# Four chained layers on one core: a second DMA queue, group norm 0 image by image, four attend banks, and setup work placed beside the convolution

## The chip, the core and the metric

One core of one Trainium2 chip runs the whole program. TensorE (PE) multiplies, VectorE (DVE) and ScalarE (ACT) work on rows of 128 partitions, GpSimd (POOL) does the roots and some elementwise work, SyncE (SP) starts transfers. The metric is the device time of one execution in microseconds; lower is better.

## The reference

The input x has 4 images of 128 channels and 16 by 16 pixels. Four layers are added to it one after another, each fed with a group norm of the running sum (32 groups of 4 channels, per image):

```
x = x + attention(gn(x))        # L0: q, k, v, softmax over 256 x 256 scores, output weights
x = x + binary_conv(gn(x))      # L1: batch norm, sign, grouped 3x3 conv with sign weights, batch norm, residual, prelu
x = x + depthwise_block(gn(x))  # L2: 3x3 depthwise conv, bn, relu, prune, 1x1 conv, bn, relu, prune
x = x + linear_attention(gn(x)) # L3: softmax(k) over pixels, context per head, output weights
```

The batch norms of L1 take mean and variance over all four images, so that each of them is a point where all images meet.

## The kernel before, in words

Everything is float32 except the operands of the binary convolution and of the filler matmuls. Channels lie on the partitions, an image is 256 columns. Each engine has one list of instructions written out by hand, and works through it in order; semaphores tie the lists together. So a wait at the head of an engine's list holds all that is behind it.

The start. SP issues four transfers on one queue: image 0, images 1 to 3 together, the early parameters (attention weights), the late parameters. DVE takes the statistics of image 0 (L722, L726, L730), PE averages them over the groups with a small matmul (L1198, `group_means`), DVE reads the result (L737, `group_out`) and forms the variance (L744), POOL takes the root (L321), DVE normalises (L750). Images 1 to 3 go through the same steps as one batch (L770 to L786, `other_group_means`, `other_roots`). On DVE the statistics of image 1 stand ahead of `group_out` of image 0.

Layer 0. For each image PE projects q, k and v (L1230, L1237, L1247), makes the scores (L1259), transposes the exponentials (L1270) and multiplies them with v (`attend`, L1283); ACT copies and exponentiates, DVE takes row maxima (L838) and adds the result to x (`x1_out`, L853). Attends 0, 1 and 2 write the same PSUM bank, so attends 1 and 2 wait until the image ahead was read by DVE.

Filler. `keep_warm(n)` is n bf16 matmuls of 256 columns whose result nobody reads (L1180).

Constants. ACT makes nine diagonal matrices of depthwise weights (`dw_diagonal`, L487) among the first steps. PE multiplies each with a mask of ones inside the image (`valid_taps`, L1310), which gives, for each pixel, the sum of the depthwise weights that fall inside; ACT copies that to `valid_sum` (`valid_taps_out`, L492). The mean of the group norm, times `valid_sum`, is taken off the depthwise result later (`mean_taps_out`, L565). `valid_taps` and images 0 and 2 of the depthwise convolution share bank 3, and `depthwise(0)` on PE begins with

```
                pe.wait_ge(x2_ready, b + 1)
                if b == 0:
                    pe.wait_ge(valid_ready, 1)
```

Layer 1. `norm1`, the first batch norm (L869 to L913), the signs (ACT, L524), four convolutions of nine taps (PE, L1296), their statistics (DVE, L919), the second batch norm, `bn2_apply` (ACT, L531), then DVE `h1_out` (L934), ACT `negative_part` (L537), DVE `x2_out` (L943).

Layer 2. PE does five taps of the depthwise convolution (L1324), ACT two (`act_tap`, L554), DVE two (L961); `group_means(2, b)` stands behind `depthwise(b)` on PE, and `group_out(2, 0)` ahead of DVE's taps and of `x2_out(3)`. Layers 2 and 3 behind that are not touched by the change.

Of the kernel before, what the change touches and what calls it, by code (L numbers as in the profile page):

```python
# [20 lines left out]
N = H * W  # L21
# [29 lines left out]
def build(nc, x, early, late, out):  # L51
# [10 lines left out]
    with ctx:  # L62
# [121 lines left out]
        o_ps = [banks[i][:, 0:N] for i in (6, 6, 6, 1)]  # L184
        setup_ps = banks[6]
# [14 lines left out]
        x_in = [sem("x_in0"), sem("x_in1")]  # L200
# [32 lines left out]
        exp_ready = sem("exp_ready")  # L233
# [52 lines left out]
        def _(pool):  # L286
# [37 lines left out]
            pool.wait_ge(var_ready[0], 1)  # L324
            root(rstd[:, 0, 0:1], ve[:, 0, 0:1]).then_inc(rstd_ready[0], 1)
            pool.wait_ge(early_in, 16)
            for i, name in enumerate(("bv", "bo")):
                ins = nc.gpsimd.tensor_scalar(bias_rows[:, i, :], ones[:, :], ep[:, EC[name]], 0.0,
                                              ALU.mult, ALU.add)
            ins.then_inc(pool_consts, 1)  # L330

            def other_roots():
                pool.wait_ge(var_ready[0], 2)
                root(rstd[:, 0, 1:B], ve[:, 0, 1:B]).then_inc(rstd_ready[0], 1)

            def x_bias(b):

                pool.wait_ge(setup_done, 2)
                pool.wait_ge(x_in[min(b, 1)], 16)
# [101 lines left out]
            x1_res_out(3)  # L441
            bn_root(1)
# [25 lines left out]
        def _(act):  # L468
            act.wait_ge(early_in, 16)
            nc.scalar.activation(bq_s[:, :], ep[:, EC["bq"]], ACT.Copy, scale=SCALE).then_inc(setup_done, 1)  # L470
            act.wait_ge(late_in, 16)
            nc.scalar.activation(conv_sign[:, :, :],
                                 lp[:, LC["conv_in"]].rearrange("p (t o) -> p t o", t=TAPS),
                                 ACT.Sign).then_inc(conv_sign_ready, 1)

            def setup_out():

                act.wait_ge(setup_mm, 1)
                nc.scalar.activation(setup[:, :, :].rearrange("p a c -> p (a c)"), setup_ps[:, 0:2 * C],
                                     ACT.Copy).then_inc(setup_done, 1)  # L480

            def dw_diagonal(tap):

                if tap == 0:
                    act.wait_ge(pool_consts, 1)
                at = LC["dw"].start + tap
# [13 lines left out]
            def softmax(b):  # L500
                act.wait_ge(nmax_ready, b + 1)
                for par in range(2):
                    nc.scalar.activation(prob[:, b, par, :], s_ps[b % 2][:, par * N:(par + 1) * N],  # L503
                                         ACT.Exp, bias=nmax[:, b, par:par + 1],
                                         accum_out=psum_rows[:, b, par:par + 1]).then_inc(exp_ready, 1)
# [101 lines left out]

            act.wait_ge(setup_done, 1)
            dw_diagonal(0)
# [3 lines left out]
            q_out(0)  # L613
# [3 lines left out]
            setup_out()  # L617
            dw_diagonal(7)
            dw_diagonal(8)
            v_out(0)  # L620
            q_out(1)
            softmax(0)
            q_out(2)
            v_out(1)
            q_out(3)
            softmax(1)
            prob_out(0)
            softmax(2)
            prob_out(1)
            softmax(3)  # L630
            prob_out(2)
            v_out(2)
            v_out(3)
            prob_out(3)
            sign_out(0)
            valid_taps_out()
            sign_out(1)
            sign_out(2)
            sign_out(3)
# [12 lines left out]
            negative_part(3)  # L652
            square_sum(2, 1)
# [43 lines left out]
        def _(dve):  # L697
# [57 lines left out]
            dve.wait_ge(x_in[0], 16)  # L755
            gn_stats(0, 0)
            gn_aggr(0, 0)
            gn_mean_sq(0, 0)
            dve.wait_ge(x_in[1], 16)
            gn_stats(0, 1)  # L760
            dve.wait_ge(pool_consts, 1)
            group_out(0, 0)
            gn_stats(0, 2)
            group_var(0, 0)
            gn_stats(0, 3)
            for b in range(1, B):
                gn_aggr(0, b)
            normalise(0, 0, t0[:, 0, :], 1)
            settle("aggr", 0, B - 1)
            step(nc.vector.tensor_tensor(msq0[:, 1:B], mv[:, 0, 1:B, 0], mv[:, 0, 1:B, 0], ALU.mult),  # L770
                 "msq0")
            settle("msq0")
            nc.vector.tensor_tensor(mv[:, 0, 1:B, 2], mv[:, 0, 1:B, 1], msq0[:, 1:B],
# [766 lines left out]
```

## Time and profile before

| | us |
|---|---|
| median of 3 runs | 76.61 |
| the 3 runs | 76.24, 78.25, 76.61 |
| span of the profiled execution, first to last instruction | 75.0 |
| PE busy, share of the span | 61.9 (83%) |
| DVE busy | 51.8 (69%) |
| ACT busy | 39.5 (53%) |
| POOL busy | 37.7 (50%) |

The page gives the profiled execution's own time as its span alone; the three runs carry no profile. The median is 1.6 us above the span. A row of the timeline gives the start, the duration, the engine, the line, the operation with its output and inputs, how many were merged, and in brackets how long the engine had been idle and what ended it.

### The profile page before, as it was taken

The numbers are of one execution on the slowest core, as the hardware profiler recorded it, in microseconds if no ns is written. First come the engines' busy times: TensorE is split into PE (matmuls) and PEld (weight loads), VectorE is DVE, ScalarE is ACT, GpSimd is POOL, SyncE is SP. The second block draws the span as 40 slices with busy tenths as digits, with TensorE's granted clock in tenths as the row PEclk, the third lists the DMA queues.
The fourth block names the chain that finished last, engine by engine and source line by source line (L and its number), as shares of the span: only waits on it lengthen the run. The fifth ranks groups of instructions, "written<-read, shape, count | busy, mean of one in ns | idle before, by whom it ended". The sixth has DMA issues, their size and how long they took to land.

```text
span 75.0 us, 1268 instructions
## 1 busy us (share of the span) xinstructions
PE 61.9 (83%) x371; PEld 50.9 (68%) x371; DVE 51.8 (69%) x179; ACT 39.5 (53%) x114; POOL 37.7 (50%) x81
## 2 busy tenths in 40 slices
PE   3993889799999999069999439949998999999930
PEld 2762778498999776046788238838775879899810
DVE  3919859674689979802262994999999998743530
ACT  5103884758945000092003889976548597977410
POOL 6605999889604547900003975999991334200000
PEclk9999999999999999975799999999999999999997
DMA  0692000000000000000000000000000000002222
GB/s 4 162 395 81 0 0 0 0 0 4 0 0 9 4 0 0 0 4 0 0 9 0 0 0 0 0 0 0 0 0 0 0 0 0 4 9 70 70 70 70
DMA packets 1415, 1.81 MB, mean 24 GB/s; under 512 B 128, under 2 KB 1152, under 8 KB 1408
## 3 DMA queue, kind: packets, MB, share of 16 engines
q1 hardware_dynamic: 1408, 1.73, 7.0%
q8 instruction: 3, 0.05, 0.2%
q14 instruction: 4, 0.03, 0.2%
HBM read 1.20 MB, written 0.52 MB: 23 GB/s over the span
## 4 chain that ended last, share of the span: by engine, by line
PE 33%; DVE 23%; issue 18%; POOL 13%; DMA 6%; ACT 3%; SPq 1%; POOLq 0%; ACTq 0%
DMA x<-in_x 6%; PE bank L1259 4%; DVE t L750 3%; PE bank L1324 3%; POOL gn_rstd L321 3%; PE bank L1347 3%; PE bank L1405 3%; POOL dw_rest L398 3%; PE bank L1385 3%; PE bank L1283 3%; DVE x L853 2%; DVE dw_acc L961 2%; POOL x_res L414 2%; PE bank L1270 2%; PE bank L1365 2%
## 5 line engine op out<-in xcount | busy, mean ns | idle before, releaser
L321 POOL TENSOR_TENSOR gn_rstd<-gn_var_eps,minus_half 128x1 f32<-128x1 f32 (+1 forms) x14 | 9.1, 651 | 13.5 <-DVE gn_var_eps L744 13.4
L1324 PE MATMUL bank<-x,dw_diag 128*128 128x256 f32 x40 | 9.5, 385 | 2.2 <-DVE x L943 2.2
L1180 PE MATMUL bank<-warm 128*128 128x256 bf16 x67 | 10.3, 314 | 1.2 <-POOL warm L306 1.2
L1324 PEld LDWEIGHTS bank<-x,dw_diag 128*128 128x128 f32 x40 | 7.3, 189 | 3.4 <-DVE x L943 2.5
L1180 PEld LDWEIGHTS bank<-warm 128*128 128x128 bf16 x67 | 7.4, 113 | 2.9 <-POOL warm L306 1.2
L1296 PE MATMUL bank<-signs,conv_blocks 128*128 128x256 bf16 x36 | 5.9, 338 | 2.6 <-ACT signs L524 2.6
L1296 PEld LDWEIGHTS bank<-signs,conv_blocks 128*128 128x128 bf16 x36 | 4.2, 118 | 4.4 <-issue 3.0
L524 ACT ACTIVATE signs<-res,bn_shift,bn_scale 128x256 bf16<-128x256 f32 x4 | 2.2, 598 | 8.2 <-DVE bn_shift L913 8.2
L919 DVE BATCH_NORM_STATS2 bn_stats<-bank 128x6 f32<-128x256 f32 x4 | 1.7, 432 | 5.4 <-PE bank L1296 5.4
L321 POOL TENSOR_TENSOR bn_rstd<-bn_var_eps,minus_half 128x1 f32<-128x1 f32 x2 | 1.2, 602 | 8.4 <-DVE bn_var_eps L929 7.8
L531 ACT ACTIVATE bn_out<-bank,bn_shift,bn_scale 128x256 f32<-128x256 f32 x4 | 2.0, 558 | 6.4 <-DVE bn_shift L913 6.4
L750 DVE TENSOR_SCALAR t<-x,gn_group,gn_rstd 128x256 f32<-128x256 f32 x8 | 4.4, 567 | 0.9 <-POOL gn_rstd L321 0.8
L1310 PE MATMUL bank<-valid,dw_diag 128*128 128x256 f32 x18 | 4.5, 388 | 0.0
L722 DVE BATCH_NORM_STATS2 gn_stats<-x 128x6 f32<-128x256 f32 x8 | 3.3, 416 | 1.7 <-DMA x<-in_x 1.7
L1259 PE MATMUL bank<-k,q 128*128 128x256 f32 x16 | 4.3, 389 | 0.2 <-DVE k L833 0.2
L1283 PE MATMUL bank<-vt,probT 128*128 128x128 f32 x32 | 4.4, 280 | 0.0
L420 POOL TENSOR_TENSOR x_h<-bn_out,x_res 128x256 f32<-128x256 f32 x4 | 3.6, 917 | 1.5 <-ACT bn_out L531 1.5
L503 ACT ACTIVATE prob<-bank,nmax 128x256 f32<-128x256 f32 x8 | 3.7, 476 | 0.8 <-DVE nmax L838 0.8
L1283 PEld LDWEIGHTS bank<-vt,probT 128*128 128x128 f32 x32 | 3.9, 192 | 0.0
L1198 PEld LDWEIGHTS bank<-gn_mean_sq,group_sum 128*128 128x128 f32 x16 | 2.6, 188 | 1.8 <-ACT squares L546 1.5
L744 DVE SCALAR_TENSOR_TENSOR gn_var_eps<-gn_group 128x1 f32<-128x1 f32 x13 | 3.6, 278 | 0.1
L838 DVE TENSOR_REDUCE nmax<-bank 128x2 f32<-128x512 f32 x4 | 2.8, 688 | 1.4 <-PE bank L1259 1.4
(151 smaller groups left out, 169.3 us busy)
## 6 DMA issues: line engine op xcount, KB each, us to landing
out<-x SPq DMA_DIRECT2D x4, 128.0 KB, 1.7
late_params<-in_late SPq DMA_DIRECT2D x1, 404.5 KB, 4.8
x<-in_x SPq DMA_DIRECT2D x1, 384.0 KB, 4.1
early_params<-in_early SPq DMA_DIRECT2D x1, 258.0 KB, 4.3
x<-in_x SPq DMA_DIRECT2D x1, 128.0 KB, 2.0
```

Of the source, the lines that this page charges most:

```text
L321: return nc.gpsimd.tensor_tensor(out_ap, in_ap, minus_half[:, 0:n], ALU.pow)
L420: nc.gpsimd.tensor_tensor(x1_h1[:, b, :], bn2_out[:, b, :], x1_res[:, b, :], ALU.add).then_inc(x1_h1_ready, 1)
L503: nc.scalar.activation(prob[:, b, par, :], s_ps[b % 2][:, par * N:(par + 1) * N], ACT.Exp, bias=nmax[:, b, par:par + 1], accum_out=psum_ro ...
L722: step(nc.vector.bn_stats(st[:, layer, b, :], xs[layer][:, b, :]), "stats", layer, b)
L744: nc.vector.scalar_tensor_tensor(out=ve[:, layer, b:b + 1], in0=g[:, 0:1], scalar=g[:, 0:1], in1=g[:, 1:2], op0=ALU.mult, op1=ALU.subtract ...
L750: nc.vector.tensor_scalar(dst, xs[layer][:, b, :], gs[:, layer, b, 0:1], rstd[:, layer, b:b + 1], ALU.subtract, ALU.mult).then_inc(t_ready ...
L1180: nc.tensor.matmul(bank[:, 0:N], warm[:, 0:C], warm[:, :], start=True, stop=True)
L1259: ins = nc.tensor.matmul(s_ps[b % 2][:, par * N:(par + 1) * N], q[:, b, par:N:2], k[:, b, :], start=True, stop=True)
L1283: ins = nc.tensor.matmul(o_ps[b][:, par * C:(par + 1) * C], probT[:, b, j, par, :], vt[:, b, j, :], start=(j == 0), stop=(j == 1))
L1296: ins = nc.tensor.matmul(conv_ps[b], conv_w[:, tap, :], signs[:, b, dy:dy + H, dx:dx + W], start=(tap == 0), stop=(tap == TAPS - 1))
L1310: ins = nc.tensor.matmul(valid_ps, dw_diag[:, tap, :], valid[:, dy:dy + H, dx:dx + W], start=(tap == 0), stop=(tap == TAPS - 1))
L1324: ins = nc.tensor.matmul(dw_ps[b], dw_diag[:, tap, :], xs[2][:, b, dy:dy + H, dx:dx + W], start=(tap == 0), stop=(tap == PE_TAPS - 1))
```

## The change

Five edits, with no change in what is computed.

1. ACT issues the early parameters on its own queue as its first instruction; SP issues image 0, image 1, images 2 and 3, and the late parameters.
2. Group norm 0 runs image by image with the same helpers as the other layers. The batch of three is gone.
3. Attends 0 to 3 write banks 6, 0, 1 and 2, so none waits for DVE's read of the one ahead; they wait for the last q, k or v to leave the bank. The softmax steps and transposes are split by halves and reordered, and the lists of PE, ACT and DVE in layer 0 are written anew.
4. The weights' fold and the bias' fold are two PSUM banks and two ACT copies.
5. Setup moves: the nine diagonals on ACT and the scale of the binary weights on DVE go behind the signs, `valid_taps` on PE behind the four convolutions, `valid_taps_out` on ACT behind `negative_part(3)`; POOL's masks and layer-2 constants go behind `x1_res_out(3)`. Filler stands where the taps were: 8, 3 and 32 ahead of the convolution, 12 instead of 33 behind.

The core of the diff:

```diff
-        o_ps = [banks[i][:, 0:N] for i in (6, 6, 6, 1)]
-        setup_ps = banks[6]
+        o_ps = [banks[i][:, 0:N] for i in (6, 0, 1, 2)]
+        fold_ps = banks[6][:, 0:C]
+        bias_ps = banks[5][:, 0:C]
...
-            sp.dma_start(xs[0][:, 1:B, :], x_v[1:B].rearrange("b c n -> c b n")).then_inc(x_in[1], 16)
-            sp.dma_start(ep[:, :], early).then_inc(early_in, 16)
+            sp.dma_start(xs[0][:, 1, :], x_v[1]).then_inc(x_in[1], 16)
+            sp.dma_start(xs[0][:, 2:B, :], x_v[2:B].rearrange("b c n -> c b n")).then_inc(x_in[2], 16)
             sp.dma_start(lp[:, :], late).then_inc(late_in, 16)
...
-            valid_mask()
-            head_masks()
-            other_roots()
+            gn_root(0, 0)
+            bias_broadcast()
+            gn_root(0, 1)
+            gn_root(0, 2)
+            gn_root(0, 3)
             x_bias(0)
             x_bias(1)
+            conv_weights()
             x_bias(2)
             x_bias(3)
-            l2_constants()
-            conv_weights()
-            sw_root()
...
             x1_res_out(2)
             x1_res_out(3)
+            valid_mask()
+            sw_root()
+            l2_constants()
+            head_masks()
             bn_root(1)
...
         def _(act):
+            act.dma_start(ep[:, :], early).then_inc(early_in, 16)
             act.wait_ge(early_in, 16)
...
+            sign_out(0)
+            sign_out(1)
+            sign_out(2)
+            sign_out(3)
             dw_diagonal(0)
...
             negative_part(3)
+            valid_taps_out()
             square_sum(2, 1)
...
             bn_shift_out(0)
+            sw_stats()
+            sw_aggr()
+            sw_variance()
+            sw_abs_sum()
             bn2_stats(0)
+            sw_scale()
+            sw_products()
...
                 pe.wait_ge(v_ready, b + 1)
                 pe.wait_ge(pt_ready, b + 1)
-                if b == 3:
+                if b == 1:
+                    pe.wait_ge(q_ready, B)
+                elif b == 2:
                     pe.wait_ge(k_ready, B)
-                elif b >= 1:
-                    pe.wait_ge(x1_ready, 2 * b)
+                elif b == 3:
+                    pe.wait_ge(v_ready, B)
...
             attend(3)
+            pe.wait_ge(exp_ready[1], B)
+            keep_warm(8)
+            group_means(1, 2)
+            keep_warm(3)
+            group_means(1, 3)
+            keep_warm(32)
+            conv(0)
+            conv(1)
+            conv(2)
+            conv(3)
             valid_taps(0)
             valid_taps(1)
-            group_means(1, 2)
             valid_taps(2)
-            group_means(1, 3)
...
             valid_taps(8)
-            conv(0)
-            conv(1)
-            conv(2)
-            conv(3)
-            keep_warm(33)
+            keep_warm(12)
             depthwise(0)
```

How the instructions move, at three places.

PE around the convolution (`bank<-valid` are the `valid_taps`, `bank<-signs` the convolution, `bank<-warm` filler, `bank<-x,dw_diag` the depthwise taps). Before:

```order
L1198 MATMUL bank<-gn_mean_sq,group_avg 128x2 [waits group_read1,stats_ready1]
L1310 MATMUL bank<-valid,dw_diag 128x256 [waits dw_diag_ready] x6
L1296 MATMUL bank<-signs,conv_blocks 128x256 [waits sign_ready,conv_w_ready]
L1296 MATMUL bank<-signs,conv_blocks 128x256 x8
...
L1296 MATMUL bank<-signs,conv_blocks 128x256 [waits sign_ready]
L1296 MATMUL bank<-signs,conv_blocks 128x256 x8
L1180 MATMUL bank<-warm 128x256 x33
L1324 MATMUL bank<-x,dw_diag 128x256 [waits valid_ready,x2_ready]
```

And now:

```order
L1204 MATMUL bank<-gn_mean_sq,group_avg 128x2 [waits group_read1,stats_ready1]
L1186 MATMUL bank<-warm 128x256 x32
L1303 MATMUL bank<-signs,conv_blocks 128x256 [waits sign_ready,conv_w_ready]
L1303 MATMUL bank<-signs,conv_blocks 128x256 x8
...
L1303 MATMUL bank<-signs,conv_blocks 128x256 [waits sign_ready]
L1303 MATMUL bank<-signs,conv_blocks 128x256 x8
L1317 MATMUL bank<-valid,dw_diag 128x256 [waits dw_diag_ready,exp_ready_odd,sum_masks]
L1317 MATMUL bank<-valid,dw_diag 128x256 [waits dw_diag_ready] x8
L1186 MATMUL bank<-warm 128x256 x12
L1331 MATMUL bank<-x,dw_diag 128x256 [waits valid_ready,x2_ready]
```

The taps of the mask went from ahead of the convolution to behind it, filler took their place, and the depthwise convolution waits for `valid_ready` as it did.

ACT from the signs to layer 2 (`valid_sum` is the copy that gives `valid_ready`, `h_neg` the negative part). Before:

```order
L524 ACTIVATE signs<-res,bn_shift,bn_scale 128x16x16 [waits t_ready1,bn_shift_ready,borders]
L492 ACTIVATE valid_sum<-bank 128x256 [waits valid_mm]
L524 ACTIVATE signs<-res,bn_shift,bn_scale 128x16x16 [waits t_ready1] x3
L531 ACTIVATE bn_out<-bank,bn_shift,bn_scale 128x256 [waits bn_shift_ready]
L531 ACTIVATE bn_out<-bank,bn_shift,bn_scale 128x256 x2
L537 ACTIVATE h_neg<-h 128x256 [waits h1_ready] x3
L531 ACTIVATE bn_out<-bank,bn_shift,bn_scale 128x256
L546 ACTIVATE squares,gn_mean_sq<-x 128x256 [waits x2_ready]
L554 ACTIVATE act_taps<-x,late_params 128x256 [waits x2_ready] x4
L537 ACTIVATE h_neg<-h 128x256 [waits h1_ready]
```

And now:

```order
L531 ACTIVATE signs<-res,bn_shift,bn_scale 128x16x16 [waits t_ready1,bn_shift_ready,borders]
L531 ACTIVATE signs<-res,bn_shift,bn_scale 128x16x16 [waits t_ready1] x3
L495 ACTIVATE dw_diag<-ident,late_params 128x128 [waits late_in,pool_consts]
L495 ACTIVATE dw_diag<-ident,late_params 128x128 x8
L538 ACTIVATE bn_out<-bank,bn_shift,bn_scale 128x256 [waits bn_shift_ready]
L538 ACTIVATE bn_out<-bank,bn_shift,bn_scale 128x256 x2
L544 ACTIVATE h_neg<-h 128x256 [waits h1_ready] x3
L538 ACTIVATE bn_out<-bank,bn_shift,bn_scale 128x256
L553 ACTIVATE squares,gn_mean_sq<-x 128x256 [waits x2_ready]
L561 ACTIVATE act_taps<-x,late_params 128x256 [waits x2_ready] x4
L544 ACTIVATE h_neg<-h 128x256 [waits h1_ready]
L500 ACTIVATE valid_sum<-bank 128x256 [waits valid_mm]
```

The copy to `valid_sum` moved from behind the first sign to behind the fourth `h_neg`, past sixteen instructions.

DVE in group norm 0 (`gn_group` is the read of the group means, `t` the normalised image). Before:

```order
L722 BN_STATS gn_stats<-x 128x6 [waits x_in1]
L737 TENSOR_TENSOR gn_group<-bank,eps_row 128x2 [waits group_ready0,pool_consts]
L722 BN_STATS gn_stats<-x 128x6
L744 SCALAR_TENSOR_TENSOR gn_var_eps<-gn_group 128x1 [waits group_read0]
L722 BN_STATS gn_stats<-x 128x6
L726 BN_AGGR gn_mean_sq<-gn_stats 128x2 [waits dve_step] x3
L750 TENSOR_SCALAR t<-x,gn_group,gn_rstd 128x256 [waits rstd_ready0]
L770 TENSOR_TENSOR gn_mean_squared<-gn_mean_sq 128x3 [waits dve_step]
L773 TENSOR_TENSOR gn_mean_sq<-gn_mean_sq,gn_mean_squared 128x3 [waits dve_step]
...
L778 TENSOR_TENSOR gn_group<-bank,eps_row 128x6 [waits group_ready0]
L783 TENSOR_TENSOR gn_mean_squared<-gn_group 128x3 [waits group_read0]
L786 TENSOR_TENSOR gn_var_eps<-gn_group,gn_mean_squared 128x3 [waits dve_step]
```

And now:

```order
L750 TENSOR_TENSOR gn_group<-bank,eps_row 128x2 [waits group_ready0,pool_consts]
L757 SCALAR_TENSOR_TENSOR gn_var_eps<-gn_group 128x1 [waits group_read0]
L735 BN_STATS gn_stats<-x 128x6 [waits x_in1]
L739 BN_AGGR gn_mean_sq<-gn_stats 128x2 [waits dve_step]
L743 SCALAR_TENSOR_TENSOR gn_mean_sq<-gn_mean_sq 128x1 [waits dve_step]
L763 TENSOR_SCALAR t<-x,gn_group,gn_rstd 128x256 [waits rstd_ready0]
L735 BN_STATS gn_stats<-x 128x6 [waits x_in23]
L750 TENSOR_TENSOR gn_group<-bank,eps_row 128x2 [waits group_ready0]
L739 BN_AGGR gn_mean_sq<-gn_stats 128x2 [waits dve_step]
L757 SCALAR_TENSOR_TENSOR gn_var_eps<-gn_group 128x1 [waits group_read0]
L743 SCALAR_TENSOR_TENSOR gn_mean_sq<-gn_mean_sq 128x1 [waits dve_step]
L814 TENSOR_SCALAR k<-bank,early_params 128x256 [waits k_mm]
```

The read of image 0's group means no longer stands behind the statistics of image 1, and images 1 to 3 have their own chain each.

## Rows read from the trace of the kernel before

**Rows 1.** The page's granted clock in forty slices, and its chain that ended last.

```profile
PEclk9999999999999999975799999999999999999997
...
PE 33%; DVE 23%; issue 18%; POOL 13%; DMA 6%; ACT 3%; SPq 1%; POOLq 0%; ACTq 0%
```

**Rows 2.** Timeline of the start: start us, us, engine, line, operation.

```profile
0.80 0.38 SPq L276 DMA_DIRECT2D x<-in_x  x1
...
1.72 0.48 SPq L278 DMA_DIRECT2D early_params<-in_early  x1
...
3.50 0.22 DVE L730 SCALAR_TENSOR_TENSOR gn_mean_sq<-gn_mean_sq 128x1 f32<-128x1 f32 x1
...
5.41 0.43 DVE L722 BATCH_NORM_STATS2 gn_stats<-x 128x6 f32<-128x256 f32 x1 [1.69 <-DMA x<-in_x]
...
5.75 0.14 DVE L737 TENSOR_TENSOR gn_group<-bank,eps_row 128x2 f32<-128x2 f32 x1
...
6.10 0.30 PEld L1205 LDWEIGHTS bank<-early_params 128*128 128x128 f32 x2 [0.94 <-DMA early_params<-in_early]
...
8.07 0.68 PE L1230 MATMUL bank<-t,early_params 128*128 128x256 f32 x2
...
10.60 2.27 DVE L750 TENSOR_SCALAR t<-x,gn_group,gn_rstd 128x256 f32<-128x256 f32 x3 [0.77 <-POOL gn_rstd L321]
```

**Rows 3.** Window of PE, layer 0: us, busy (matmuls), granted clock, DMA share, GB/s.

```profile
8.07:25.13 17.06, 16.25 (x107) 1.00 0.01 2
```

**Rows 4.** Chain that ended last, in layer 0: start us, us, engine, line, pieces.

```profile
16.41 0.86 PE bank L1259 x4
...
17.27 0.44 PE bank L1270 x4
...
19.09 0.89 PE bank L1283 x8
```

**Rows 5.** Timeline from the last attend to the second batch norm.

```profile
23.99 1.14 PE L1283 MATMUL bank<-vt,probT 128*128 128x128 f32 x8
...
26.88 0.38 PE L1198 MATMUL bank<-gn_mean_sq,group_avg 128*128 128x2 f32 x2
...
31.82 0.60 ACT L524 ACTIVATE signs<-res,bn_shift,bn_scale 128x256 bf16<-128x256 f32 x1 [8.17 <-DVE bn_shift L913]
...
32.57 5.86 PE L1296 MATMUL bank<-signs,conv_blocks 128*128 128x256 bf16 x36 [2.61 <-ACT signs L524]
...
38.26 3.77 PE L1180 MATMUL bank<-warm 128*128 128x256 bf16 x33
...
39.52 0.55 POOL L321 TENSOR_TENSOR bn_rstd<-bn_var_eps,minus_half 128x1 f32<-128x1 f32 x1 [7.80 <-DVE bn_var_eps L929]
```

**Rows 6.** Windows of PE around the convolution, columns as in group 3.

```profile
33.00:33.50 0.50, 0.50 (x5) 0.50 0.06 16
...
36.00:36.50 0.50, 0.50 (x5) 0.61 0.00 0
```

**Rows 7.** Windows of POOL in layer 0, over its masks and layer-2 constants, columns as in group 3.

```profile
7.69:9.73 2.04, 1.84 (x8) 1.00 0.00 0
13.55:15.51 1.96, 1.64 (x7) 1.00 0.00 0
```

**Rows 8.** Timeline from the second batch norm into the depthwise convolution.

```profile
32.33 0.36 ACT L492 ACTIVATE valid_sum<-bank 128x256 f32<-128x256 f32 x1
...
40.56 1.48 ACT L531 ACTIVATE bn_out<-bank,bn_shift,bn_scale 128x256 f32<-128x256 f32 x3 [6.39 <-DVE bn_shift L913]
...
44.25 2.43 PE L1324 MATMUL bank<-x,dw_diag 128*128 128x256 f32 x10 [2.22 <-DVE x L943]
...
46.24 0.41 ACT L537 ACTIVATE h_neg<-h 128x256 f32<-128x256 f32 x1
...
46.83 0.16 DVE L737 TENSOR_TENSOR gn_group<-bank,eps_row 128x2 f32<-128x2 f32 x1 [1.02 <-PE bank L1198]
...
47.44 0.47 DVE L961 SCALAR_TENSOR_TENSOR dw_acc<-x,late_params,act_sum 128x256 f32<-128x256 f32 x1
```

More of the change, by code:

```diff
@@ L321, in root, with bias_broadcast @@
                 return nc.gpsimd.tensor_tensor(out_ap, in_ap, minus_half[:, 0:n], ALU.pow)
[L324 to L334, printed above, removed]
+            def bias_broadcast():
+                pool.wait_ge(early_in, 16)
+                for i, name in enumerate(("bv", "bo")):
+                    ins = nc.gpsimd.tensor_scalar(bias_rows[:, i, :], ones[:, :], ep[:, EC[name]], 0.0,
+                                                  ALU.mult, ALU.add)
+                ins.then_inc(pool_consts, 1)
             def x_bias(b):
-                pool.wait_ge(setup_done, 2)
-                pool.wait_ge(x_in[min(b, 1)], 16)
+                pool.wait_ge(setup_done, 3)
+                pool.wait_ge(x_in[min(b, 2)], 16)
                 nc.gpsimd.tensor_tensor(xb[:, b, :].rearrange("p (a c) -> p a c", a=2),
@@ L498, in q_out, with softmax @@
                                      bias=bq_s[:, :], scale=SCALE).then_inc(q_ready, 1)
-            def softmax(b):
+            def softmax(b, par):
                 act.wait_ge(nmax_ready, b + 1)
[L502 to L505, printed above, removed]
+                nc.scalar.activation(prob[:, b, par, :], s_ps[b % 2][:, par * N:(par + 1) * N],
+                                     ACT.Exp, bias=nmax[:, b, par:par + 1],
+                                     accum_out=psum_rows[:, b, par:par + 1]).then_inc(exp_ready[par], 1)
             def v_out(b):
@@ L842, in rinv_out @@
             def rinv_out(b):
-                dve.wait_ge(exp_ready, 2 * b + 2)
+                for par in range(2):
+                    dve.wait_ge(exp_ready[par], b + 1)
                 step(nc.vector.reciprocal(rinv[:, b, :], psum_rows[:, b, :]), "rinv", b)
@@ L1034, in x4_out @@
                                                op0=ALU.add, op1=ALU.add).then_inc(x4_ready, 1)
-            sw_stats()
-            sw_aggr()
-            other_group_vars()
-            sw_variance()
+            x_arrived(0)
+            gn_stats(0, 0)
+            gn_aggr(0, 0)
+            gn_mean_sq(0, 0)
+            dve.wait_ge(pool_consts, 1)
+            group_out(0, 0)
+            group_var(0, 0)
+            x_arrived(1)
+            gn_stats(0, 1)
+            gn_aggr(0, 1)
+            gn_mean_sq(0, 1)
+            norm0(0)
+            x_arrived(2)
+            gn_stats(0, 2)
+            group_out(0, 1)
+            gn_aggr(0, 2)
+            group_var(0, 1)
+            gn_mean_sq(0, 2)
             k_out(0)
-            sw_abs_sum()
             norm0(1)
-            norm0(2)
+            group_out(0, 2)
+            group_var(0, 2)
+            gn_stats(0, 3)
+            k_out(1)
+            gn_aggr(0, 3)
+            norm0(2)
+            gn_mean_sq(0, 3)
+            row_max(0)
+            group_out(0, 3)
+            group_var(0, 3)
+            row_max(1)
             norm0(3)
-            row_max(0)
-            k_out(1)
+            k_out(2)
+            k_out(3)
             rinv_out(0)
-            k_out(2)
-            row_max(1)
-            k_out(3)
             row_max(2)
+            row_max(3)
+            x1_out(0)
             rinv_out(1)
-            row_max(3)
-            rinv_out(2)
-            x1_out(0)
             x1_stats(0)
-            sw_scale()
             gn_aggr(1, 0)
             gn_mean_sq(1, 0)
-            sw_products()
-            rinv_out(3)
-            x1_out(1)
-            group_out(1, 0)
-            group_var(1, 0)
-            x1_stats(1)
-            gn_aggr(1, 1)
-            gn_mean_sq(1, 1)
+            x1_out(1)
+            x1_stats(1)
+            group_out(1, 0)
+            gn_aggr(1, 1)
+            group_var(1, 0)
+            gn_mean_sq(1, 1)
+            rinv_out(2)
+            rinv_out(3)
             norm1(0)
```

189 lines of the change are left out of this document (86 added, 103 removed).

## The prediction

> **What bounds the kernel now.** I read the page's chain of waits first, then the timeline of the start, the windows of PE, and the timelines around the three places where work moves. The chain [rows 1] belongs to no single engine: PE has 33% of it, DVE 23%, POOL 13%, and 18% is "issue", most of which is one piece across the binary convolution, where the chain lost its track. So each stretch has its own limit, and there are four of them.
>
> Start, to 8.07: nothing but a chain of small steps. Image 0's statistics are complete at 3.50 + 0.22 = 3.72, but DVE reads its group means only at 5.75, because its list has the statistics of image 1 ahead, and these waited 1.69 us for images 1 to 3 to land. The first q projection starts at 8.07 [rows 2]. The early parameters are there at 6.10 [rows 2].
>
> Layer 0, 8.07 to 25.13: PE, busy 16.25 of 17.06 us [rows 3], with a hole about the normalisation of images 1 to 3, which starts only at 10.60 after POOL's root [rows 2].
>
> First batch norm to the convolution, 25.13 to 32.57: DVE and POOL. PE has nothing to do after the mask taps and stands 2.61 us [rows 5]. Its clock falls behind that: the windows show 0.50 (1.2 GHz) from 33.00 and 0.61 in the one at 36.00, the page's slices the same [rows 1, 6]. So from 33.0 to 36.4, some 3.4 us, PE ran at half speed, all of it inside the convolution.
>
> Second batch norm to layer 2: DVE and POOL again, until the depthwise convolution starts at 44.25, as soon as x2 of image 0 is written [rows 8]. There PE had stood 2.22 us, and its clock stayed at 2.4 GHz [rows 1, 8].
>
> **The change, part by part.**
>
> *Start.* DVE can read image 0's group means one group matmul behind 3.72. Such a matmul takes 0.38 us [rows 5], with hand-overs some 0.6, so 4.3 in place of 5.75 [rows 2]. From that read to the first projection it takes 8.07 - 5.75 = 2.3 us now; I keep it, which gives 6.6, and take off 0.1 for the batched group means that PE no longer has ahead: the projections start at 6.5. The early parameters must be there by then; they are at 6.10 even from third place, and are issued at 0.80 or so in place of 1.72 [rows 2]. Bounds: 6.2 if the steps are tighter, 7.3 if image 0 itself comes late.
>
> *Layer 0.* PE's work for one image: scores 0.86, transposes 0.44, attend 0.89 [rows 4]; a q or k projection is two passes of the same 256 columns as the four of the scores, 0.43 each, and v is four passes of 128 columns like the transposes, 0.44. That is 3.49, and 14.0 for four. The bias fold (0.44, four passes of that size) and five group means (0.2 of PE's time each, estimated as half the row's 0.38 [rows 5]) bring 15.4. With no hole at all attend(3) would end at 6.5 + 15.4 = 21.9, with the holes of today at 6.5 + 17.1 = 23.6, against 25.13. The gain lies between 3.2 and 1.5 us. The four banks take away the wait of attend on DVE, and image 1 no longer waits for the batch, but norm0(3) stands behind row_max(1) in DVE's new list and new holes will open there. I take 2.5.
>
> *Up to the signs.* The chain from x1_out(3) to the first sign is DVE's and POOL's and has the same instructions in the same order. Filler of 8 stands where two taps stood, so the two last group means find PE free. No change.
>
> *Convolution.* The 32 fillers start behind group_means(1, 3), which ends at 26.88 + 0.38 = 27.26 [rows 5] on today's clock. One takes 3.77/33 = 0.11 us, so they end at 30.8, and PE stands 1.8 us until 32.57. That is less than the 2.22 us which left the clock alone, so I expect full speed. The convolution took 38.26 - 32.57 = 5.7 us [rows 5]; 36 passes of 256 bf16 columns at the filler's 0.11 take 4.0. Gain 1.7; bounds 0 (it falls all the same) and 1.7.
>
> *What is put beside it.* POOL gets 2.04 + 1.96 us of masks and constants [rows 7] and a root of 0.55 [rows 5], 4.6 in all, from about the first sign on. It is needed again for the batch norm's root, 39.52 - 31.82 = 7.7 us behind the first sign today, 6.0 then. Hidden, with 1.4 us to spare. ACT's nine diagonals lie between the fourth sign (some 2.4 us behind the first) and bn2_apply (40.56 - 31.82 - 1.7 = 7.0 behind it); at no more than 0.5 us each, which is what a merged bn2_apply takes [rows 8], they need 4.5 of 4.6. Hidden, barely. DVE's seven small operations, 0.22 or less like the row of L730 [rows 2], fit ahead of the first and second statistics, while PE convolves. Cost of all three: nothing; if a cover went, some tenths.
>
> *Depthwise convolution, the price.* depthwise(0) waits for valid_ready as before. The copy that gives it stood at 32.33 [rows 8] and now stands behind negative_part(3), which ends at 46.24 + 0.41 = 46.65 on today's clock. It takes 0.36, so depthwise(0) starts at 47.0 and not at 44.25 [rows 8]: 2.8 us later. Behind it on PE is group_means(2, 0), on which DVE waits with group_out(2, 0) (already 1.02 us today), and behind that in DVE's list stand its own taps and x2_out(3). So nearly all is passed on. What comes back is DVE's wait between 46.83 and 47.44 for POOL's sum of ACT's taps, 0.4 us, since that sum will be there. Net +2.4; bounds 1.5 and 2.8.
>
> *Its clock.* PE's work behind the first sign: 0.75 until the convolution starts, 4.0 for it, 18 passes of the taps at 0.86/4 = 0.215, or 3.9, 12 fillers, 1.3: done after 9.9 us. The depthwise convolution starts 7.0 + (47.0 - 40.56) = 13.5 behind the first sign. PE stands 3.5 us, longer than the 2.61 (3.0 to the fall) that cost the clock. I expect 1.2 GHz: the fall can come 0.5 us before the restart, so that 2.9 of 3.4 slow microseconds hold work, half of which is lost: +1.4. Bounds 0 and 1.7, the last being the price in the convolution.
>
> **Sum**, against the span of 75.0: -2.5 - 1.7 + 2.4 + 1.4 = -0.4, so 74.6. The median of the runs is 1.6 above the span, and the three differ by 2.0. I add 1.6: **76.2 us**.
>
> **The second queue, page against trace.** Image 0 is issued at 0.80 and the early parameters 0.92 later [rows 2]; with two queues both start together. Early's 258 KB landed 0.69 us behind images 1 to 3 [rows 2], so they cost the engines about that long. The Trainium skill, "DMA: Bandwidth & Descriptors", section "Issuing engines are not separate DMA queues", says that transfers issued from several engines end up on the same 16 DMA engines and interleave, which saves only issuing time. By that rule image 0 shares from the start and comes late, which speaks against this edit; the rows above cannot show it, since there is one queue in them.
>
> **Rivals.**
>
> *B, the clock stays up in the depthwise convolution.* For it: the evidence is two stalls, 2.22 and 2.61 us, and in both the work ahead counted too. Against it: 3.5 us is longer than either. Without the 1.4: 74.8 us.
>
> *C, image 0 late.* If image 0 waits for all of early's data, the start moves by 0.7: 76.9 us. For it: nothing orders the two queues. Against it: the order of need is the order of issue for the rest.
>
> *D, slower: DVE's fixed order eats layer 0.* DVE now has four short chains woven with k_out and row_max, and each step waits for PE or POOL. norm0(3) stands behind row_max(1), that behind scores(1), so q, k and v of image 3 can start only after them; every late piece holds all behind it. The point from which it decides: if attend(3) ends at 24.8 or later, only 0.3 of the 2.5 is left, and the rest of the sum gives 75.0 - 0.3 - 1.7 + 2.4 + 1.4 = 76.8, or 78.4 us. Against it: today's PE is 95% busy there, so DVE has had room.
>
> *E, the depthwise delay is covered.* If negative_part(3) comes earlier than today, or DVE is late anyway, only 1.0 of the 2.4 stays: 74.8 with the slow clock.
>
> **Numbers.** Forecast 0.45, B 0.20, C 0.12, D 0.13, E 0.10. The range reaches from 74.3 (B or E with half a microsecond more from layer 0) to 77.7 (the forecast with the lower bound of layer 0, or C with some of it); beyond lie most of D and little of the rest. 2% is 1.5 us, about what a measurement of this kernel can tell from no change. Faster by more than that, under 75.1: B and E and a small part of the forecast, 0.35. Slower, over 78.1: D and a tail, 0.15. Within: 0.50.
>
> **What would show it.** The first projection at about 6.5, attend(3) ending near 22.6. Granted clock 1.00 through the convolution, the first filler behind the taps 8 us behind the first conv matmul. depthwise(0) released by ACT's valid_sum and not by DVE's x, some 6.4 us behind bn2_apply(0) in place of 3.7. Granted clock 0.50 in the first two depthwise images. Wrong would be: depthwise(0) released by x2, a clock of 0.50 in the convolution, attend(3) after 23.6, or PE waiting on dw_diag in the taps.

## The result: slower by 5%

The median is 80.53 us over 4 runs (79.69 to 80.95), against 76.50 over 4 for the kernel before (76.24 to 78.25): a ratio of 1.052, with a 95% interval of 1.045 to 1.059. This ratio and the others below compare only the runs within 1.5% of each kernel's fastest, while the medians take all runs. The forecast was 76.2 and the range ended at 77.7. The profiled execution took 80.95 us with a span of 79.1, which is 4.1 longer than the span of before.

The page of the changed kernel: the span, the granted clock in forty slices and the chain that ended last.

```profile
span 79.1 us, 1332 instructions
...
PEclk9999999999999999999999996599999999999999
...
PE 46%; DVE 18%; POOL 13%; issue 8%; ACT 8%; DMA 4%; POOLq 0%; ACTq 0%
```

PE has 46% of the chain and had 33% [rows 1]. The slow slices of the clock have gone from the convolution to slices 25 and 26, the depthwise convolution. By this line the first half of the program ran at full clock. It did not, as the next rows show.

The start of the changed kernel, from its timeline: start us, us, engine, line, operation, and in brackets the idle time and what ended it.

```profile
0.80 0.40 ACTq L470 DMA_DIRECT2D early_params<-in_early  x1
...
1.17 2.53 PE L1186 MATMUL bank<-warm 128*128 128x256 bf16 x11 [1.17 <-POOL warm L307]
...
4.07 0.43 DVE L735 BATCH_NORM_STATS2 gn_stats<-x 128x6 f32<-128x256 f32 x1 [1.10 <-DMA x<-in_x]
...
5.11 0.56 PE L1204 MATMUL bank<-gn_mean_sq,group_avg 128*128 128x2 f32 x2 [1.41 <-DVE gn_mean_sq L743]
...
5.78 0.16 DVE L750 TENSOR_TENSOR gn_group<-bank,eps_row 128x2 f32<-128x2 f32 x1 [0.81 <-PE bank L1204]
...
7.52 1.20 PE L1237 MATMUL bank<-t,early_params 128*128 128x256 f32 x2
```

The statistics of image 0 end, with L743, at 4.96; before they ended at 3.72 [rows 2]. Their wait ends on the transfer of x. PE's eleven fillers are over at 3.70, and it stands 1.41 us. And the first projection takes 1.20 us for two passes, where before it took 0.68 [rows 2].

How long single matmuls took (ns, min/median/max, first and last start). The changed kernel, fillers of the first 8 us and scores of layer 0:

```profile
L1186 PE MATMUL bank<-warm x17: 374/421/421, 1.2 to 7.0; 128*128 128x256 bf16 x17
...
L1260 PE MATMUL bank<-k,q x16: 379/379/634, 12.4 to 20.4; 128*128 128x256 f32 x16
```

The kernel before, fillers behind its convolution:

```profile
L1180 PE MATMUL bank<-warm x33: 272/273/273, 38.3 to 41.8; 128*128 128x256 bf16 x33
```

The same filler took 273 ns at a granted clock of 1.00 (2.4 GHz) and 421 ns here. Single matmuls overlap, so a row of them tells more: the first eleven fillers took 2.53 us, 0.23 each, and the 33 of the kernel before 3.77 us, 0.11 each [rows 5]. The first scores take up to 634 ns, the rest 379. So PE ran at 1.2 GHz at first. The windows say nothing of it:

```profile
7.50:14.00 6.50, 6.50 (x19) 1.00 0.00 0
...
48.15:51.50 3.35, 3.35 (x10) 0.50 0.00 0
```

The record of the clock begins at its first change. Here that change is the rise at 14.01; what lies ahead of it is printed as 1.00, though a duration contradicts it. Only 19 matmuls fit into 6.50 busy microseconds; between 14.00 and 26.70 there are 93 in 12.70.

The changed kernel from the last attend to the depthwise convolution, its timeline:

```profile
25.53 1.14 PE L1290 MATMUL bank<-vt,probT 128*128 128x128 f32 x8
...
28.93 3.65 PE L1186 MATMUL bank<-warm 128*128 128x256 bf16 x32
...
33.62 2.08 ACT L531 ACTIVATE signs<-res,bn_shift,bn_scale 128x256 bf16<-128x256 f32 x4 [8.33 <-DVE bn_shift L895]
...
40.76 1.48 ACT L538 ACTIVATE bn_out<-bank,bn_shift,bn_scale 128x256 f32<-128x256 f32 x3 [2.44 <-DVE bn_shift L895]
...
46.75 0.36 ACT L500 ACTIVATE valid_sum<-bank 128x256 f32<-128x256 f32 x1
...
47.25 3.74 PE L1331 MATMUL bank<-x,dw_diag 128*128 128x256 f32 x10 [3.42 <-ACT valid_sum L500]
...
50.78 0.43 PE L1204 MATMUL bank<-gn_mean_sq,group_sum 128*128 128x2 f32 x2
...
51.25 0.16 DVE L750 TENSOR_TENSOR gn_group<-bank,eps_row 128x2 f32<-128x2 f32 x1 [5.24 <-PE bank L1204]
```

Against [rows 5, 8]: attend(3) ends at 26.67 and not at 25.13 (+1.5); the first sign stands at 33.62 and not at 31.82 (+1.8); bn2_apply at 40.76 and not at 40.56 (+0.2, so the convolution gave 1.6); the depthwise convolution 6.5 behind it and not 3.7 (+2.8); DVE's read of the group means 4.00 behind the first depthwise matmul and not 2.58 (+1.4). At that point the kernel is 4.4 late, and 4.1 at its end. Two losses of some 1.5 and 4.2 us, then, and one gain.

### The profile page after: what moved, and what is told of

Read it like the earlier page. It is cut to its first block, busy times and chain, and to the rows that moved or that the text cites. A ratio compares the mean times of both kernels' runs of the same rounds, so it can differ in the third digit from the quotient of the medians.

```text
span 79.1 us, 1332 instructions
## 1 busy us (share of the span) xinstructions
PE 66.7 (84%) x393; PEld 56.0 (71%) x393; DVE 51.5 (65%) x183; ACT 39.8 (50%) x115; POOL 38.5 (49%) x83
## 4 chain that ended last, share of the span: by engine, by line
PE 46%; DVE 18%; POOL 13%; issue 8%; ACT 8%; DMA 4%; POOLq 0%; ACTq 0%
PE bank L1260 6%; PE bank L1331 5%; DMA x<-in_x 4%; PE bank L1237 4%; PE bank L1228 3%; PE bank L1186 3%; PE bank L1204 3%; PE bank L1354 3%; PE bank L1412 3%; POOL dw_rest L395 2%; PE bank L1247 2%; PE bank L1392 2%; DVE dw_acc L943 2%; DVE x L835 2%; PE bank L1290 2%
## 5 line engine op out<-in xcount | busy, mean ns | idle before, releaser
L322 POOL TENSOR_TENSOR gn_rstd<-gn_var_eps,minus_half 128x1 f32<-128x1 f32 x16 | 9.9, 620 | 23.1 <-DVE gn_var_eps L757 23.1
L1331 PE MATMUL bank<-x,dw_diag 128*128 128x256 f32 x40 | 11.1, 430 | 3.4 <-ACT valid_sum L500 3.4
L1186 PE MATMUL bank<-warm 128*128 128x256 bf16 x85 | 12.6, 301 | 1.2 <-POOL warm L307 1.2
L1186 PEld LDWEIGHTS bank<-warm 128*128 128x128 bf16 x85 | 9.1, 110 | 3.0 <-POOL warm L307 1.2
L750 DVE TENSOR_TENSOR gn_group<-bank,eps_row 128x2 f32<-128x2 f32 x16 | 2.5, 155 | 7.0 <-PE bank L1204 7.0
L1303 PE MATMUL bank<-signs,conv_blocks 128*128 128x256 bf16 x36 | 4.3, 276 | 1.8 <-ACT signs L531 1.8
L1204 PEld LDWEIGHTS bank<-gn_mean_sq,group_avg 128*128 128x128 f32 x16 | 3.3, 238 | 3.2 <-issue 1.9
L505 ACT ACTIVATE q<-bank,bq_scaled 128x256 f32<-128x256 f32 x4 | 1.9, 474 | 5.6 <-PE bank L1228 5.6
L1204 PE MATMUL bank<-gn_mean_sq,group_avg 128*128 128x2 f32 x16 | 3.1, 261 | 1.8 <-DVE gn_mean_sq L743 1.7
L1204 PEld LDWEIGHTS bank<-gn_mean_sq,group_sum 128*128 128x128 f32 x16 | 2.9, 207 | 1.5 <-ACT squares L553 1.0
L561 ACT ACTIVATE act_taps<-x,late_params 128x256 f32<-128x256 f32 x8 | 3.6, 494 | 0.5 <-DVE x L925 0.5
```

What stands on the lines that cost most here:

```text
L322: return nc.gpsimd.tensor_tensor(out_ap, in_ap, minus_half[:, 0:n], ALU.pow)
L561: nc.scalar.activation(act_taps[:, b, i, :].rearrange("p (h w) -> p h w", h=H), xs[2][:, b, dy:dy + H, dx:dx + W], ACT.Copy, scale=lp[:, L ...
L1186: nc.tensor.matmul(bank[:, 0:N], warm[:, 0:C], warm[:, :], start=True, stop=True)
L1204: nc.tensor.matmul(gn_ps[:, 0:2], (group_avg if layer < 2 else group_sum)[:, :], mv[:, layer, b, 0:3:2], start=True, stop=True).then_inc(g ...
L1303: ins = nc.tensor.matmul(conv_ps[b], conv_w[:, tap, :], signs[:, b, dy:dy + H, dx:dx + W], start=(tap == 0), stop=(tap == TAPS - 1))
L1331: ins = nc.tensor.matmul(dw_ps[b], dw_diag[:, tap, :], xs[2][:, b, dy:dy + H, dx:dx + W], start=(tap == 0), stop=(tap == PE_TAPS - 1))
```

## Experiments

The theory, after reading this: (1) the copy to `valid_sum` costs 2.8 us of wait and the clock behind it; (2) layer 0 lost because the second queue brings image 0 late, and because the fillers end before it is there, which keeps PE at 1.2 GHz. The rival for (2) is D of the prediction: DVE's new order holds layer 0 up. Each run stands beside runs of the kernel before on the same chip. The first four had a median of 76.12 us beside them (7 runs, 74.54 to 77.66), the other four 76.17 (17 runs, 74.53 to 78.20). The kernel before thus moves by 3.7 us from run to run. Its mean granted clock was 1.00 in its fastest run and 0.93 in its slowest, but at a mean of 0.97 it took anything from 74.70 to 78.02, so that mean alone doesn't give the time. Each trace below is of one execution.

**More filler at the start, both queues kept.**

```diff
             pe.wait_ge(warm_ready, 1)
-            keep_warm(11)
+            keep_warm(17)
             pe.wait_ge(gn_consts, 1)
```

> The changed kernel with 17 instead of 11 fillers ahead of the first group means, so that PE works on until image 0's statistics are there (4.96 in its profile; 17 fillers at 0.23 us from 1.17 end at 5.05). Theory (PE ran at 1.2 GHz until 14.0 because its fillers ended at 3.7 while image 0 landed late): filler durations fall from 421 to 273 ns by about 7 us, the q, k and score matmuls of images 0 and 1 halve, attend(3) ends some 3 us earlier, and the time falls from 80.5 to about 77.2 us. Rival (DVE's fixed order holds layer 0, whatever the clock): no change, 80.0 to 81.0.

Median 77.76 us (76.15 to 78.05, 4 runs). The profiled one, 76.15, in its timeline:

```profile
1.17 3.76 PE L1186 MATMUL bank<-warm 128*128 128x256 bf16 x17 [1.17 <-POOL warm L307]
...
5.03 0.35 PE L1204 MATMUL bank<-gn_mean_sq,group_avg 128*128 128x2 f32 x2
...
7.12 0.70 PE L1237 MATMUL bank<-t,early_params 128*128 128x256 f32 x2
...
22.18 1.14 PE L1290 MATMUL bank<-vt,probT 128*128 128x128 f32 x8
...
43.43 0.36 ACT L500 ACTIVATE valid_sum<-bank 128x256 f32<-128x256 f32 x1
...
43.94 2.40 PE L1331 MATMUL bank<-x,dw_diag 128*128 128x256 f32 x10 [3.43 <-ACT valid_sum L500]
```

Image 0 is as late as before (its statistics start at 3.98), but PE stands only 0.10 us ahead of L1204, the first projection starts at 7.12 and takes 0.70, and attend(3) ends at 23.32, 3.35 us earlier. DVE's order is the same as in the changed kernel, so D is not what held layer 0. The gain of 2.8 us in the median is a little under the 3.3 expected. PE stands 3.43 us ahead of the depthwise convolution as in the changed kernel, and here its clock did not fall: ten matmuls took 2.40 and not 3.74. The other three runs, without a profile, took 77.60 to 78.05, 1.45 to 1.9 more, at a mean clock of 0.98. That is about the price of a slow depthwise convolution, 1.4 in the changed kernel; that they had one is not shown.

**One queue again**: the early parameters third on SP's queue, behind images 2 and 3.

```diff
             sp.dma_start(xs[0][:, 2:B, :], x_v[2:B].rearrange("b c n -> c b n")).then_inc(x_in[2], 16)
+            sp.dma_start(ep[:, :], early).then_inc(early_in, 16)
             sp.dma_start(lp[:, :], late).then_inc(late_in, 16)
...
         def _(act):
-            act.dma_start(ep[:, :], early).then_inc(early_in, 16)
             act.wait_ge(early_in, 16)
```

> The changed kernel with the early parameters back on SP's queue, behind images 2 and 3. Theory (the second queue made image 0 late): image 0's statistics start at 2.9 as in the kernel before, not at 4.07; the 11 fillers then reach the group means without a hole, the clock rises near 6, and the time is about 77.0 us. Rival (the late image has another cause, such as splitting the transfer of images 1 to 3): statistics at 4.0, time 80.5. If the image is early and the clock stays down all the same, about 79.5.

Median 78.90 us (78.51 to 79.40, 4 runs). Its timeline:

```profile
2.89 0.43 DVE L735 BATCH_NORM_STATS2 gn_stats<-x 128x6 f32<-128x256 f32 x1
...
3.93 0.56 PE L1204 MATMUL bank<-gn_mean_sq,group_avg 128*128 128x2 f32 x2 [0.24 <-DVE gn_mean_sq L743]
...
6.77 1.20 PE L1237 MATMUL bank<-t,early_params 128*128 128x256 f32 x2
...
22.74 1.14 PE L1290 MATMUL bank<-vt,probT 128*128 128x128 f32 x8
...
44.50 4.61 PE L1331 MATMUL bank<-x,dw_diag 128*128 128x256 f32 x10 [3.43 <-ACT valid_sum L500]
```

Image 0 comes 1.18 us earlier. The clock is still at 1.2 GHz at the first projection (1.20), but rises at 9.09 and not at 14.01; attend(3) ends at 23.88. Of these 2.8 us, 0.85 are lost again, since the depthwise convolution was slow for longer (4.61 for its first ten). The result lies between the expectations: with the image in time, eleven fillers still leave PE standing 0.24 us and the clock rises late. The queue alone accounts for the image's lateness, for 0.75 us of the first projection's start (6.77, not 7.52) and for a part of the clock.

**The copy earlier**: `valid_taps_out` between the second and the third negative part.

```diff
             negative_part(1)
+            valid_taps_out()
             negative_part(2)
...
             negative_part(3)
-            valid_taps_out()
```

> The changed kernel with ACT's valid_sum copy between negative_part(1) and negative_part(2) instead of behind negative_part(3). Theory (depthwise(0) waits for this copy, and PE's stall lowers its clock): the depthwise convolution starts 3.7 us behind bn2_apply(0), as before, not 6.5; granted clock 1.00 in it; the time falls by 2.8 + 1.3 = 4.1, to about 76.4 us. Rival (DVE or ACT hold that stage anyway): a fall of 1 us or less.

Median 75.75 us (74.20 to 76.10, 4 runs), 4.8 under the changed kernel. Its timeline:

```profile
39.96 1.48 ACT L538 ACTIVATE bn_out<-bank,bn_shift,bn_scale 128x256 f32<-128x256 f32 x3 [2.44 <-DVE bn_shift L895]
...
42.20 0.37 ACT L500 ACTIVATE valid_sum<-bank 128x256 f32<-128x256 f32 x1
...
43.65 2.43 PE L1331 MATMUL bank<-x,dw_diag 128*128 128x256 f32 x10 [0.62 <-DVE x L925]
```

The depthwise convolution starts 3.7 behind bn2_apply as it did before the change, released by x2 and not by `valid_sum`, at full clock. That is 4.1 of the 4.8. The rest is layer 0, where the clock rose at 12.04 in this execution and attend(3) ended 0.8 earlier, though the start is the same code, image 0 came 0.3 later and PE stood longer ahead of its group means, 1.70 us.

**The second queue put into the kernel before**, its other side.

```diff
-            sp.dma_start(ep[:, :], early).then_inc(early_in, 16)
...
         def _(act):
+            act.dma_start(ep[:, :], early).then_inc(early_in, 16)
             act.wait_ge(early_in, 16)
```

> The kernel before with one edit, the early parameters issued by ACT as its first instruction. Theory (the second queue delays image 0 by about 1.1 us; it costs by the hole behind the fillers, not by itself): image 0's statistics at 4.0 instead of 2.9; its 14 fillers end at 4.3 and the group means come at 5.0, so the hole is 0.7 us. If the clock still rises near 6, the time is within 0.5 of 76.5, since DVE waits there for images 1 to 3 anyway; if this hole is enough to keep it down, 78.5 to 80. Rival (the second queue is harmless): statistics at 2.9, 76.5 or a little less.

Median 78.16 us (75.71 to 78.49, 4 runs), 2.0 over the kernel before; its one run near full clock, 75.71, is 1.2 over that of the kernel before, 74.54. Its statistics of image 0 start at 3.92. From its timeline:

```profile
4.97 0.35 PE L1198 MATMUL bank<-gn_mean_sq,group_avg 128*128 128x2 f32 x2 [0.77 <-DVE gn_mean_sq L730]
...
7.64 0.59 PE L1222 MATMUL bank<-gn_mean_sq,group_avg 128*128 128x6 f32 x2 [1.31 <-DVE gn_mean_sq L773]
8.09 1.20 PE L1230 MATMUL bank<-t,early_params 128*128 128x256 f32 x2
```

And its windows of PE (us, busy and matmuls, granted clock, DMA share, GB/s):

```profile
4.00:7.30 3.30, 1.56 (x13) 1.00 0.50 190
7.30:14.10 6.80, 6.46 (x20) 0.50 0.00 0
```

The lateness reaches every step of the chain, PE stands twice, 0.77 and 1.31 us. The clock was not kept down here: it rose at 3.91, before the first stall, and the record has a fall at 7.33 that lasts to 14.15. This run also closes the reading above: the same two passes take 1.20 us here at a recorded 0.50, and 1.20 us in the changed kernel at a printed 1.00.

**Filler ahead of the convolution, in the kernel before**: 16 between the mask taps and `conv(0)`, to cut its stall of 2.61 us [rows 5].

```diff
             valid_taps(8)
+            keep_warm(16)
             conv(0)
```

> The kernel before with 16 fillers between the last mask tap and the first convolution, nothing else. Theory (the convolution's 1.7 us were the clock alone, and filler in the hole gives them back): PE's hole of 2.61 us ahead of the convolution shrinks to 0.9, the convolution takes 4.1 instead of 5.7 us in every run, and the median falls by about 1.6, to 74.6 us. Rival (the clock at the convolution goes by when it last changed, not by the hole): part of the runs still at 76.1.

Median 74.94 us (74.48 to 76.02, 10 runs) against 76.17. The ratio is 1.003 (0.998 to 1.007), so among the fastest runs of both there is no difference. The gain is in how often the slower ones come. No run of ten was above 76.02; of the seventeen of the kernel before, ten were. From its timeline:

```profile
32.14 4.26 PE L1296 MATMUL bank<-signs,conv_blocks 128*128 128x256 bf16 x36 [0.87 <-ACT signs L524]
...
42.22 3.45 PE L1324 MATMUL bank<-x,dw_diag 128*128 128x256 f32 x10 [2.21 <-DVE x L943]
```

The stall is 0.87, and the convolution takes 4.26 where it took 5.86 [rows 5]; the median fell by 1.2 us, with 1.6 expected. But in this execution the clock fell in the depthwise convolution (0.50 from 43.46), behind a stall of 2.21 us that had left it alone in the profile of before (2.22, [rows 8]). So the stall's length alone doesn't decide.

**Less filler at the start, in the kernel before**: one queue and image 0 in time, but a hole of 1.3 us on PE.

```diff
             pe.wait_ge(warm_ready, 1)
-            keep_warm(14)
+            keep_warm(6)
```

> The kernel before with 6 instead of 14 fillers ahead of the first group means, which leaves a hole of 1.4 us on PE, as long as the one in the changed kernel. Theory (the hole alone keeps PE at 1.2 GHz into layer 0, whatever the order of the work): matmuls of layer 0 are slow until 9 or later, attend(3) ends 1 to 3 us later and the median is 77.5 to 79.0 us. Rival (the changed kernel's slow clock came of its other edits): 76.1.

Median 77.50 us (76.62 to 77.76, 4 runs), ratio 1.036 (1.021 to 1.051). Its timeline:

```profile
3.92 0.56 PE L1198 MATMUL bank<-gn_mean_sq,group_avg 128*128 128x2 f32 x2 [1.30 <-DVE gn_mean_sq L730]
...
7.86 1.20 PE L1230 MATMUL bank<-t,early_params 128*128 128x256 f32 x2
...
24.22 1.14 PE L1283 MATMUL bank<-vt,probT 128*128 128x128 f32 x8
```

With no transfer late, and no edit but the fillers, PE is at 1.2 GHz in the first projection (1.20); the clock rose at 11.77, against 5.67 in the profile of before. The median is 1.3 over that of the kernel before. In the profiled execution, itself the fastest of the four, attend(3) ended only 0.2 later than in the profile of before, so this shows the hole's effect on the clock better than its price. In the old order layer 0 had stalls of its own (PE busy 16.25 of 17.06 us [rows 3]), which could take in a part of the slow matmuls; that is argued, no run shows it by itself.

**Both repairs**: 17 fillers and the copy early, two queues kept.

> The changed kernel with both mends so far: 17 fillers at the start and valid_sum's copy between negative_part(1) and negative_part(2); the second queue stays. Theory (two separate causes whose prices add): 80.5 less 3.3 for the clock in layer 0 and less 2.8 to 4.1 for the depthwise stage, 73.2 to 74.4 us, thus about 2 under the kernel before. Rival (they overlap, DVE takes over as the bound once layer 0 is faster): 75.5 or more.

Median 73.84 us (73.68 to 73.85, 4 runs), ratio to the kernel before 0.988 (0.985 to 0.992). The two repairs took 2.8 and 4.8 singly, 6.7 together, 0.9 less than their sum; 0.8 of the 4.8 was layer 0's, in the profiled run.

**All three**: one queue, the copy early, and filler of 13, 6 and 3 at the start.

```diff
             pe.wait_ge(warm_ready, 1)
-            keep_warm(11)
+            keep_warm(13)
             pe.wait_ge(gn_consts, 1)
             group_means(0, 0)
-            keep_warm(4)
+            keep_warm(6)
             fold_weights()
-            keep_warm(2)
+            keep_warm(3)
```

> The changed kernel with one queue again, valid_sum's copy early, and 13, 6 and 3 fillers in place of 11, 4 and 2 at the start so that PE has no hole before the first projection. Theory: image 0 is there 1.1 us earlier than with two queues, the clock rises by 7 at the latest, the first projection starts near 6.6, attend(3) ends near 22.6 as first forecast, and the time is 72.8 to 73.8 us, the fastest of all. Rival (the early parameters, then at 5.4, or DVE's order hold it): same as the kernel with two queues and both mends.

Median 73.22 us (72.78 to 73.81, 6 runs), ratio 0.981 (0.971 to 0.991), the lowest median of all; its slowest runs are as long as those with two queues. Its timeline:

```profile
2.88 0.43 DVE L735 BATCH_NORM_STATS2 gn_stats<-x 128x6 f32<-128x256 f32 x1
...
3.93 0.43 PE L1204 MATMUL bank<-gn_mean_sq,group_avg 128*128 128x2 f32 x2
...
6.34 0.68 PE L1237 MATMUL bank<-t,early_params 128*128 128x256 f32 x2
...
21.39 1.14 PE L1290 MATMUL bank<-vt,probT 128*128 128x128 f32 x8
...
30.26 4.26 PE L1303 MATMUL bank<-signs,conv_blocks 128*128 128x256 bf16 x36 [1.81 <-ACT signs L531]
...
36.65 1.47 ACT L538 ACTIVATE bn_out<-bank,bn_shift,bn_scale 128x256 f32<-128x256 f32 x3 [2.43 <-DVE bn_shift L895]
...
40.33 2.43 PE L1331 MATMUL bank<-x,dw_diag 128*128 128x256 f32 x10 [0.62 <-DVE x L925]
```

Attend(3) ends at 22.53, 4.14 earlier than in the changed kernel, and from bn2_apply to the end of the first ten depthwise matmuls the 4.1 of the third experiment come back: 8.2 in all. The profiled executions differ by 80.95 - 72.78 = 8.17.

## Why the prediction was wrong, step by step

The sum was -2.5 - 1.7 + 2.4 + 1.4 = -0.4 on the span; the trace has +4.1. Three terms held, and one had the wrong sign.

| step | forecast | measured |
|---|---|---|
| start and layer 0 | -2.5 | +1.5 at attend(3) |
| up to the signs | 0 | +0.3 |
| convolution at full clock | -1.7 | -1.6 |
| depthwise(0) waits for `valid_sum` | +2.8, less 0.4 behind it | +2.8, less 0.3 |
| its clock | +1.4 | +1.4 |

*Start and layer 0: the step that failed* is "the projections start at 6.5", and with it the unspoken assumption that PE has 2.4 GHz from there on, through the 2.5 us of gain in layer 0. They started at 7.52, beyond the bound of 7.3 that I had written down for a late image 0, and at half the clock. Split by the runs: from 7.52 to the end of attend(3) the changed kernel took 19.15 us; with all three repairs it took 22.53 - 6.34 = 16.2. So the clock cost 3.0, and the late start 1.2. That is the 4.1 between the two, and the forecast missed by 4.0. Six traces with the new order of layer 0 bear the split out (us):

| kernel | PE stands ahead of the first group means | clock rises at | first projection to end of attend(3) |
|---|---|---|---|
| all three repairs | 0 | 4.09 | 16.19 |
| 17 fillers | 0.10 | 4.75 | 16.20 |
| both repairs | 0.13 | 6.50 | 16.20 |
| one queue | 0.24 | 9.09 | 17.11 |
| copy early | 1.70 | 12.04 | 18.04 |
| changed kernel | 1.41 | 14.01 | 19.15 |

Each microsecond at 1.2 GHz behind the first projection cost about 0.4. Of the late start's 1.2, some 0.75 is the queue's: the start moves from 7.52 to 6.77 with one queue and nothing else changed. The remaining 0.4 goes with the slow clock ahead of the projection: with 17 fillers, two queues and nearly the same lateness it starts at 7.12.

With a clean start, attend(3) ends at 22.53, and I had 22.6 for it. That the two agree is in part luck. I had counted 15.4 us of PE's work and chosen 16.1 for the stretch, to leave room for new holes. The window of PE in the kernel with all three repairs shows no hole, and the work is 0.8 more than counted:

```profile
6.34:22.53 16.19, 16.19 (x113) 1.00 0.00 1
```

The gain of 2.5 thus came, at 2.6, in a kernel with one queue and more filler. How it divides between group norm 0 image by image, the four banks and the new order no run shows. I read in [rows 2] that the steps of the start hang on each other and never asked what PE does while they are late. The change said it in plain sight: fewer fillers at the start (11, 4 and 2, for 14, 5 and 2), and a second transfer beside the first.

*The second queue.* Both edits of it are in the traces: image 0's statistics at 2.88 with one queue and 3.92 to 4.35 with two, in either kernel. The rule of the Trainium skill that the prediction weighed ("DMA: Bandwidth & Descriptors", section "Issuing engines are not separate DMA queues") is borne out. Between 2 and 4 us the trace of the changed kernel has all 144 packets of ACT's queue and 297 of SP's, and its page has 3.4 us from issue to landing for the first two images, 128 KB each, and 3.5 for the early parameters; in the kernel before image 0 took 2.0. Rival C, built on it, named the right mechanism and put 0.7 us on it. For the start by itself that was close (0.75). What it left out was the price that hung on the lateness: the clock.

*Rival D* fell, as the run with 17 fillers shows, though the sign that the prediction gave for it came: attend(3) ended behind 24.8. A late end of attend(3) doesn't tell DVE's order from a slow PE. A trace of D is in the 0.3 up to the signs: DVE still has image 2's statistics (from 26.52) when attend(3) ends, and takes its result 0.42 behind it; in the trace of before it is 0.15.

*Convolution.* The stall was 1.8 as forecast, the clock 1.00 throughout. What was put beside it was hidden: POOL's last head mask ended at 38.0, 1.7 ahead of its root, and PE never waited for `dw_diag`: ACT's nine diagonals took 2.72 us, not 4.5.

*Depthwise convolution.* It was released by `valid_sum` 6.5 behind bn2_apply (forecast 6.4), and moving that one copy gave it back. This was the prediction's surest term, a wait read off the order of ACT's list.

*Its clock.* Right in the profile (0.50 from 48.15 to 51.56), but less sure than it looked: with the same stall of 3.43 us the clock fell in the changed kernel and with one queue, and stayed up in the profiled run with 17 fillers. Rival B happened there. So the forecast that it would fall was partly luck.

*What stays open.* When the clock falls or rises relative to the work differs between executions of one kernel: the same instructions at the start gave a rise at 14.01 and at 12.04, and stalls of 2.2 and 3.4 us each went both ways. What PE must do to be sure of it these runs don't settle. They show only that the repaired kernels vary less: 3.7 us between the fastest and the slowest of 17 runs of the kernel before, 1.0 in 6 runs with all three repairs, 0.2 in 4 runs with two.

## What to carry to other kernels

Where filler keeps an engine's clock up, count it as a part of the path: set its end against the time at which the awaited data now arrives, and do so again for every edit that shifts that arrival, because here PE stood 1.4 us and paid 3.0 more in clock. A short operation that was moved out of the way costs what stands in front of it in its new place; look for its reader before moving it, and put it ahead of work that waits anyway. Before giving a second queue to a transfer that is needed later, ask what it takes from the one that is needed first; here that was 0.75 us of the start, and no run shows a gain from it.

## What the runs showed of the hardware that was not expected

- The granted clock is printed as 1.00 ahead of its first recorded change, whatever it was. Durations tell: a filler of 256 bf16 columns takes 421 ns at 1.2 GHz and 273 at 2.4.
- In the three traces with a hole of 1.3 to 1.7 us behind the first fillers the clock rose only at 11.8 to 14.0 us, though PE was busy without a break from 7.2 to 7.5 on. In the five whose fillers reached the group means within 0.13 us (two of them in the old order) it rose at 4.1 to 6.5. The longest hole did not go with the latest rise. With a hole of 0.24 us, one queue and eleven fillers, the rise came at 9.09; whether that small hole did it is not shown.
- The price of a slow clock depends on what else the engine waits for. Of the time at 1.2 GHz behind the first projection, the new order of layer 0 lost 0.39 to 0.45 us per microsecond; the old order lost 0.24 with two queues (rise at 14.15) and 0.11 with less filler (rise at 11.77).
- A transfer of 258 KB, issued at the same moment on another queue, put off the first use of a 128 KB image by 1.0 to 1.2 us in four of the five kernels that had it, and by 1.5 in the fifth (2.88 to 4.35). In the kernel before, where it was the only edit, the image's way from issue to landing went from 2.0 to 3.1 us.
